# Four cond layers: ternary weights in two passes, chain scalars one per row, later waits for vectors, and other order tables for layers 0 and 1

## The chip, the cores and the metric

The kernel runs on one core of a Trainium2 chip. The metric is the time of one execution on the device in microseconds. The core has five engines with their own instruction streams: TensorE (PE, matrix products and transpositions), VectorE (DVE), ScalarE (ACT), GpSimd (POOL) and SyncE (SP, which issues most DMAs). They meet through semaphores.

## The reference

Input x has 8 examples of 512 tokens and 256 channels, and a condition vector of 256 for each example. Four layers follow one another on x. What matters here is layer 0 with its weights, and layer 1.

```
weight_quant(w): scale = 1 / max(mean|w|, 1e-5);  clip(round(w * scale), -1, 1) / scale
act_quant(x):    scale = 127 / max(max|x| over the row, 1e-5);  clip(round(x * scale), -128, 127) / scale
bitlinear(x, w, nw, b): xn = x * rsqrt(mean(x^2) + 1e-8) * nw;  act_quant(xn) @ weight_quant(w).T (+ b)

layer 0:  h = bitlinear(silu(c), wa0);  h = bitlinear(silu(gate) * y, wa2) with gate, y = bitlinear(h, wa1)
          h = rmsnorm(bitlinear(h, wa3) + ba3) * wr;  six vectors per example = bitlinear(h, wa4) + ba4
          mx = layernorm(x) * (1 + sc) + s;  i, f, g = bitlinear(mx, wi / wf / wg)
          o = scan(silu(i) * (1 - f), f) over the tokens;  x += gate_mix * bitlinear(rmsnorm(o) * silu(g), wo)
          x += gate_mlp * hgrn_mlp(layernorm(x) modulated)   with wm1 (256 to 2048) and wm2 (1024 to 256)
layer 1:  x += ffn(rmsnorm(merge(x, a mean of four tokens after pre_w, mixed with a style vector)))
```

So every weight matrix of layer 0 is made ternary (-1, 0 or 1, times its mean absolute value) by the kernel itself. wa0 to wa4 act on the 8 condition vectors, wi to wm2 on x. Layer 2 is an attention layer, layer 3 a state space layer; the change leaves both as they are.

## The kernel before

**Setup (`setup`, line 130).** SP loads wa0 to wa4 and then wi, wf, wg, wo, wm1, wm2 as f32, 128 partitions wide. A matrix is cut into pieces of at most 1536 columns (`pieces_of`). For each matrix ScalarE takes the sum of absolute values of each piece (`absolute`, L264) except for wm1, whose sums VectorE takes (L517). `inverse` (L374 to L378) adds up the pieces, lets TensorE sum over the partitions (L300) and makes the mean and its inverse. ScalarE multiplies the piece by the inverse (`scaled`, L270), VectorE adds and subtracts a large constant, which rounds (`whole`, L386), and then clips to -1 and 1 (`clipped`, L391). The codes are bf16.

Between these goes the chain of the condition: for each of wa0 to wa4 `front` (squares, multiplication with the norm vector, largest absolute value), `peak` (L424, L426), a power of -0.5 on GpSimd (L248), `quantised` (L435 to L446), the product on TensorE and `taken` (L453). The mean square, its root and the scales are tiles of 128 partitions and 8 columns, one column for each example, the same in each partition. The result, six vectors for each example, is written to DRAM (mod0).

**Layers 0 and 1 (`layers01`, line 583).** Both layers run in one block, example after example, in software pipelining. Five tables, `SP_TURN`, `POOL_TURN`, `ACT_TURN`, `PE_TURN` and `DVE_TURN`, each list the stages of its engine. An entry (stage, t, ahead) says that in turn b the engine does part t of that stage for example b + ahead. `steps` walks through the table turn by turn and leaves out examples that do not exist. An engine does its instructions in this order and waits at each for its semaphores. The stages of an example are, for layer 0: stats, root, xl, mx, ssq, rms, xw, amax, qs, xq (transposition), qT, proj, fi, scan, o, u, xo, yo, add1, x1; then the MLP with stats2 up to xq2, qT2, gate, up, silu, h, hq, qhT, y2, add2, x2; for layer 1: ssq3, xn, turn, xT, pre, z, fold, dots, s, base, merge, yn, turn2, hT, f1, gelu, f2, x3. The stage setup of layer 1 (harmonics, style) is done once, for example 0. On TensorE it is the first entry that has an example and waits for twelve small loads.

At the start of the block SP issues seven loads of norm vectors (ni, nf, ng, gn, no_, nm1, nm2), then mod_norm of example 0, the twelve small loads, and three weight loads. VectorE and GpSimd wait for all seven vectors before their first stage (L1145 and L742).

Of the kernel before, what the change touches and what calls it, by code (L numbers as in the profile page):

```python
# [11 lines left out]
P = 128  # L12
ALU = mybir.AluOpType
# [5 lines left out]
B, L, D = 8, 512, 256  # L19
# [96 lines left out]
WM1 = len(COND_W) + 4  # L116

# [7 lines left out]
def piece_number(i, j):  # L125

    return sum(len(pieces_of(q)) for q in range(i)) + j


def setup(nc, io, main, mean, ident, mod0, x_res, x_loaded):  # L130

    groups = COND_W + MAIN_W
    with ExitStack() as ctx:
# [11 lines left out]
        first4 = sb("first4", [P, PIECE], BF16)  # L145
# [11 lines left out]
        def codes(i, a, z):  # L157

            if i == 4:
                return first4[:] if a == 0 else raw4[:, a - PIECE:a].bitcast(BF16)[:, 0:PIECE]  # L160
            return (tern[i] if i < 4 else main[i - 5])[:, a:z]
# [4 lines left out]
        ones, half = sb("ones", [P, P]), sb("half", [P, B])  # L166
# [4 lines left out]
        sqk, pmax, ms, rms, s4, s6, s5 = [sb(name, [P, B]) for name in ("sqk", "pmax", "ms", "rms", "s4", "s6", "s5")]  # L171
        top, diag, own5, out_scale = sb("top", [B, 1]), sb("diag", [B, B]), sb("own5", [B, B]), sb("out_scale", [B, 1])
# [16 lines left out]
        def every(tile, k):  # L189
            return tile[:].rearrange("p (a b) -> p a b", a=1).to_broadcast([P, k, B])  # L190
# [4 lines left out]
        half_ready, ones_ready, ident_cleared, ident_ready = sem("half_ready"), sem("ones_ready"), sem("ident_cleared"), sem("ident_ready")  # L195
        abs_summed, abs_summed_v, asum_ready, total_ready, mean_ready, inv_ready = (
            sem("abs_summed"), sem("abs_summed_v"), sem("asum_ready"), sem("total_ready"), sem("mean_ready"), sem("inv_ready"))
        scaled_up, rounded, code_ready = sem("scaled_up"), sem("rounded"), sem("code_ready")
# [4 lines left out]
        top_ready, diag_ready, max_ready, ms_ready, rms_ready = (  # L203
            sem("top_ready"), sem("diag_ready"), sem("max_ready"), sem("ms_ready"), sem("rms_ready"))
        scale_step, s6_ready, s5_ready, qv_step, q_ready, y_ready, y_taken = (
            sem("scale_step"), sem("s6_ready"), sem("s5_ready"), sem("qv_step"), sem("q_ready"), sem("y_ready"), sem("y_taken"))
        tail_step, own_step, ba4_step, params_ready, stored = sem("tail_step"), sem("own_step"), sem("ba4_step"), sem("params_ready"), sem("stored")

        with nc.Block() as block:
            @block.sync  # L210
            def _(sp):
# [6 lines left out]
                a = 0  # L218
                for name, k in VECTORS:
                    sp.dma_start(rows[a:a + k, :], io["L0_cond_" + name].rearrange("(k p) -> k p", p=P)).then_inc(rows_loaded, 16)  # L220
                    a += k
                for i in (1, 2, 3):
                    weight(i)
# [6 lines left out]
                sp.wait_ge(rounded, piece_number(4, 0))  # L230
# [6 lines left out]
            def _(pool):  # L237
# [5 lines left out]
                                 pattern=[[-1, P]], channel_multiplier=1).then_inc(ident_ready, 1)  # L243
                gp.memset(half[:], -0.5).then_inc(half_ready, 1)
# [6 lines left out]
            def _(act):  # L251
# [3 lines left out]
                def absolute(i):  # L255
# [3 lines left out]
                    for j, (a, z) in enumerate(pieces_of(i)):  # L259
# [14 lines left out]
                absolute(0)  # L274
                scaled(0)
                absolute(1)
                absolute(2)
                scaled(1)
                scaled(2)
                absolute(3)  # L280
                act.wait_ge(h_ready, 2)
                ac.activation(h[:, 0:KA * B], h[:, 0:KA * B], ACT.Silu).then_inc(gate_ready, 1)
                scaled(3)
                absolute(4)
                scaled(4)
                for i in range(5, 9):
                    absolute(i)
# [2157 lines left out]
```

## Time and profile before

| what | us |
|---|---|
| median of 3 runs (2211.11 to 2214.26) | 2212.96 |
| the profiled execution's own time | 2210.04 |
| its span, first to last instruction | 2208.3 |
| TensorE busy | 1845.4 (84%) |
| VectorE busy | 1373.1 (62%) |
| ScalarE busy | 1121.4 (51%) |
| GpSimd busy | 601.9 (27%) |

The profile is one execution. "Busy" is the time in which an engine works on an instruction; a wait for a semaphore isn't busy. The timeline gives for each instruction its start, its duration, engine, line, the output and the inputs by tile names, and how long the engine was idle before it and who released it. Two times are told apart: the duration of an instruction, and the distance to the start of the next one, which is somewhat shorter where the next does not depend on it.

### The profile page before, as it was taken

How to read it: one execution, taken by the hardware profiler on the slowest of the kernel's cores; microseconds unless marked ns; L12 is line 12 of the kernel's file. 1: busy time of each engine (PE TensorE's matmuls, PEld its weight loads, DVE VectorE, ACT ScalarE, POOL GpSimd, SP SyncE). 2: the span in 40 equal slices, each digit the busy share in tenths (PEclk: the TensorE clock that was granted, in tenths of full speed). 3: DMA queues.
4: the chain of work that ended last, by engine and by line, in shares of the span. 5: the costliest groups of instructions: out<-in, count | busy, mean ns of one | idle time of the engine just before them, and what ended most of it. 6: DMA issues, size and time to landing. Idle time of an engine off the chain costs nothing. (4 is left out here: it accounts for less than half of the span.)

```text
span 2208.3 us, 26216 instructions
## 1 busy us (share of the span) xinstructions
PE 1845.4 (84%) x8726; PEld 1102.0 (50%) x8748; DVE 1373.1 (62%) x2936; ACT 1121.4 (51%) x2131; POOL 601.9 (27%) x774
## 2 busy tenths in 40 slices
PE   2244678988989997588999999999999857899998
PEld 1022445666666665422435454544544435566666
DVE  4647788798788642587776867686875205333331
ACT  7546567767767642215666665657576510121121
POOL 1056665565664421200001010110101100233322
PEclk9756799999999999759999999999999986899999
DMA  9310000000000001402112030202030011000000
GB/s 359 96 65 5 15 18 1 18 18 1 18 13 3 8 3 39 106 2 60 39 26 60 4 60 4 60 4 62 3 63 4 3 47 49 1 19 10 19 10 20
DMA packets 88313, 78.21 MB, mean 35 GB/s; under 512 B 9969, under 2 KB 82122, under 8 KB 87922
## 3 DMA queue, kind: packets, MB, share of 16 engines
q1 hardware_dynamic: 88178, 76.52, 12.7%
q8 instruction: 71, 1.16, 0.2%
q14 instruction: 64, 0.52, 0.1%
HBM read 46.67 MB, written 4.27 MB: 23 GB/s over the span
## 5 line engine op out<-in xcount | busy, mean ns | idle before, releaser
L1845 DVE TENSOR_REDUCE l_small<-l_psum 128x1 f32<-128x512 f32 x512 | 330.0, 685 | 135.3 <-PE l_psum L1792 130.8
L1604 ACT ACTIVATE l_prob<-l_psum 128x512 f32<-128x512 f32 x512 | 286.4, 596 | 227.2 <-PE l_psum L1662 223.9
L1792 PE MATMUL l_psum<-l_kT,l_qT 96*128 96x512 bf16 x512 | 191.3, 410 | 27.3 <-DMA l_kT<-l_early 12.2
L1662 PE MATMUL l_psum<-l_qT,l_kT 99*128 99x512 bf16 x512 | 174.4, 385 | 16.0 <-ACT l_prob L1604 14.3
L1588 POOL TENSOR_TENSOR k_x_res<-k_x_res,l_add 128x256 f32<-128x256 f32 x32 | 23.2, 726 | 466.9 <-DVE l_add L1889 466.9
L1671 PE MATMUL l_psum<-l_prob,l_v 128*32 128x512 f32 x1024 | 138.1, 612 | 0.2
L1792 PEld LDWEIGHTS l_psum<-l_kT,l_qT 96*128 96x128 bf16 x512 | 49.4, 98 | 171.1 <-DVE l_small L1845 116.6
L1736 PE MATMUL l_psum<-l_w,l_gu 128*128 128x256 f32 x512 | 133.9, 390 | 0.7 <-ACT l_gu L1620 0.7
L94 PE MATMUL l_psum<-l_hT,l_w 128*128 128x512 f32 x256 | 116.7, 606 | 8.6 <-ACT l_hT L2199 8.6
L94 PE MATMUL l_psum<-l_turned_over,l_w 128*128 128x512 f32 x256 | 120.3, 596 | 4.2 <-ACT l_gu L1620 4.2
L94 PE MATMUL l_psum<-l_hT,l_w_f 128*128 128x512 f32 x256 | 118.8, 600 | 2.7 <-ACT l_gu L965 1.7
L1125 PE MATMUL l_psum<-l_w_f,l_gu 128*128 128x256 f32 x512 | 120.1, 381 | 0.8 <-ACT l_gu L965 0.8
L94 PE MATMUL l_psum<-l_w,l_gu 128*128 128x256 f32 x512 | 111.9, 379 | 0.8 <-ACT l_gu L2203 0.8
L1736 PEld LDWEIGHTS l_psum<-l_w,l_gu 128*128 128x128 f32 x512 | 96.9, 195 | 19.2 <-ACT l_gu L1620 1.5
L94 PEld LDWEIGHTS l_psum<-l_w,l_gu 128*128 128x128 f32 x512 | 96.7, 190 | 14.4 <-ACT l_gu L2203 1.6
L1125 PEld LDWEIGHTS l_psum<-l_w_f,l_gu 128*128 128x128 f32 x512 | 94.1, 190 | 14.3 <-ACT l_gu L965 1.6
L1662 PEld LDWEIGHTS l_psum<-l_qT,l_kT 99*128 99x128 bf16 x512 | 46.4, 98 | 108.6 <-ACT l_prob L1604 63.4
L2203 ACT ACTIVATE l_gu<-l_psum,l_b 128x512 f32<-128x512 f32 x64 | 44.0, 687 | 96.2 <-PE l_psum L94 96.2
L94 PE MATMUL l_psum<-l_w_qkv,l_xT 128*128 128x512 f32 (+1 forms) x256 | 88.8, 490 | 3.2 <-DVE l_xn L1907 1.9
L2199 ACT ACTIVATE l_hT<-l_psum,l_shift,l_scale 128x512 f32<-128x512 f32 x16 | 11.7, 773 | 156.3 <-PE l_psum L100 156.2
L94 PEld LDWEIGHTS l_psum<-l_hT,l_w 128*128 128x128 f32 x256 | 48.4, 194 | 66.2 <-issue 55.6
L94 PE MATMUL l_psum<-k_t_wm,l_qT 128*128 128x512 bf16 x234 | 71.2, 406 | 10.8 <-DVE l_h L1260 3.4
(388 smaller groups left out, 3972.1 us busy)
## 6 DMA issues: line engine op xcount, KB each, us to landing
su_raw<-in_L_cond_wa SPq DMA_DIRECT2D x6, 1536.0 KB, 21.6
l_qT<-l_early SPq DMA_DIRECT2D x32, 192.0 KB, 3.6
l_kT<-l_early SPq DMA_DIRECT2D x32, 192.0 KB, 3.3
k_x_res<-in_x SPq DMA_DIRECT2D x1, 4096.0 KB
l_w<-in_L_cond_W SPq DMA_DIRECT2D x4, 1024.0 KB, 12.6
l_qT<-l_early SPq DMA_DIRECT2D x32, 128.0 KB, 3.2
l_kT<-l_early SPq DMA_DIRECT2D x32, 128.0 KB, 3.1
out<-k_x_res SPq DMA_DIRECT2D x8, 512.0 KB, 2.9
```

Source lines behind the costliest of these rows:

```text
L94: last = nc.tensor.matmul(out, w, m, start=(i == 0), stop=(i == len(pairs) - 1), **kw)
L1125: last = pe.matmul(psum[:, 6 + i % 2, 0:D], gu[:, f, tok(i)], w_f2[:, f, :], start=(f == 0), stop=(f == KF - 1))
L1588: pool.tensor_tensor(x_tile(e, n), x_tile(e, n), add2[:], ALU.add).then_inc(x_ready.sem, 1)
L1604: act.activation(prob[:, s % 2, j, :], psum[:, 2 + n % 2, :], ACT.Exp, scale=float(HD) ** -0.5).then_inc(exp_ready.sem, 1)
L1662: pe.matmul(psum[:, 2 + n % 2, :], kT[e % 2][:, head, tok(s % T)], qT[e % 2][:, head, :], start=True, stop=True).then_inc(st_ready.sem, 1)
L1671: last = pe.matmul(psum[j * BLOCK:(j + 1) * BLOCK, 4, :], v[e % 2][:, kt, at:at + BLOCK], prob[:, n % 2, j, :], start=(kt == 0), stop=(kt ...
L1736: last = pe.matmul(psum[:, mlp_bank(e, t), 0:D], gu[:, f, tok(t)], w_2[:, f, :], start=(f == 0), stop=(f == KF - 1))
L1792: pe.matmul(psum[:, n % 2, :], qT[e % 2][0:SROWS, n // T, tok(n % T)], kT[e % 2][0:SROWS, n // T, :], start=True, stop=True).then_inc(s_re ...
L1845: dve.tensor_reduce(mx[:, n % T, n // T:n // T + 1], psum[:, n % 2, :], AX.X, ALU.max).then_inc(max_ready.sem, 1)
L2199: act.activation(dst[:, k, :], psum[:, bank + k, :], ACT.Identity, scale=scale[:, k, bass.ds(nxt, 1)], bias=shift[:, k, bass.ds(nxt, 1)]). ...
L2203: act.activation(gu[:, n, :], psum[:, n % 2, :], ACT.Gelu_apprx_tanh, bias=b_1[:, n:n + 1]).then_inc(gu_ready.sem, 1)
```

## The change

**Setup.** For wa0 to wa3 VectorE does all of the ternary work in three passes: `whole` multiplies by the inverse mean and adds the large constant, in place and in f32; `low` subtracts it and takes the minimum with 1; `clipped` takes the maximum with -1. For wa4 and the weights of layer 0 VectorE does `whole`, and ScalarE takes the sign of the piece minus the constant (`sign`, with the tile `back` as bias), which is the code. The first two pieces of wa4 go to a tile of their own. VectorE takes the absolute sums of wm1 and wm2, between pieces of wa4. The inverses of wi, wf, wg and wo are made in one go. The norm vectors' seven row loads are issued by ScalarE instead of SP, before its first activation. In the chain the mean square, root and scales are now one value on each of 8 partitions; two diagonals (for the quantising scale and the output scale) are spread to all partitions by one product on TensorE (`scales`, `spread`). The mean square is taken before the largest value. x is loaded once `low` is through wa3.

**Layers 0 and 1.** mod_norm of example 0 is loaded first, then the seven vectors. VectorE waits for the three ifg vectors at the first xw and for the other four at the first xw2, GpSimd for these four at the first sgn. All five tables have the same stages in another order, with other values of ahead; layer 0 runs up to 4 turns ahead in place of 3, and ScalarE's table has gelu in two groups.

```diff
-                def scaled(i):
-                    act.wait_ge(inv_ready, i + 1)
-                    for a, z in pieces_of(i):
-                        ac.activation(raw[i][:, a:z], raw[i][:, a:z], ACT.Copy, scale=inv[:, i:i + 1]).then_inc(scaled_up, 1)
+                def sign(i):
+                    for j, (a, z) in enumerate(pieces_of(i)):
+                        act.wait_ge(rounded, piece_number(i, j) + 1)
+                        if i == 4 and j >= 2:
+                            act.wait_ge(signed, sign_number(i, j - 2) + 1)
+                        ac.activation(codes(i, a, z), raw[i][:, a:z], ACT.Sign, bias=back[:]).then_inc(signed, 1)
+                a = 0
+                for name, k in VECTORS:
+                    act.dma_start(rows[a:a + k, :], io["L0_cond_" + name].rearrange("(k p) -> k p", p=P)).then_inc(rows_loaded, 16)
+                    a += k
...
                 def whole(i, j):
                     a, z = pieces_of(i)[j]
-                    dve.wait_ge(scaled_up, piece_number(i, j) + 1)
-                    V.tensor_scalar(codes(i, a, z), raw[i][:, a:z], ROUND, ROUND, ALU.add, ALU.subtract).then_inc(rounded, 1)
+                    V.tensor_scalar(raw[i][:, a:z], raw[i][:, a:z], inv[:, i:i + 1], ROUND, ALU.mult, ALU.add).then_inc(rounded, 1)
+                def low(i, j):
+                    a, z = pieces_of(i)[j]
+                    dve.wait_ge(rounded, piece_number(i, j) + 1)
+                    V.tensor_scalar(codes(i, a, z), raw[i][:, a:z], ROUND, 1.0, ALU.subtract, ALU.min).then_inc(lowered, 1)
                 def clipped(i, j):
-                    V.tensor_scalar(codes(i, a, z), codes(i, a, z), 1.0, -1.0, ALU.min, ALU.max).then_inc(code_ready, 1)
+                    V.tensor_scalar(codes(i, a, z), codes(i, a, z), -1.0, None, ALU.max).then_inc(clipped_ready, 1)
...
+                def scales(i, n):
+                    step = Chain(dve, scale_step, i, 3)
+                    dve.wait_ge(top_ready, i + 1)
+                    dve.wait_ge(rms_ready, n + 1)
+                    step.link(V.tensor_tensor(s4[:], top[:], rms[:], ALU.mult))
+                    step.link(V.tensor_scalar(s4[:], s4[:], 1e-5, 1.0 / 127.0, ALU.max, ALU.mult))
+                    if i < 4:
+                        V.tensor_scalar(s5[:], s4[:], mean[0:B, i:i + 1], None, ALU.mult).then_inc(s5_ready, 1)
+                    step.link(V.reciprocal(s6[:], s4[:]))
+                    step.close()
+                    V.tensor_tensor(s6[:], s6[:], rms[:], ALU.mult).then_inc(s6_ready, 1)
+                    if i < 4:
+                        dve.wait_ge(s5_ready, i + 1)
+                        V.tensor_scalar(diag[:, B:2 * B], ident[0:B, 0:B], s5[:], None, ALU.mult)
+                    dve.wait_ge(s6_ready, i + 1)
+                    V.tensor_scalar(diag[:, 0:B], ident[0:B, 0:B], s6[:], None, ALU.mult).then_inc(diag_ready, 1)
...
-                dve.wait_ge(vectors_loaded, 16 * 7)
                 for stage, t, e in steps(DVE_TURN):
...
                     elif stage == "xw":
+                        if e == 0 and t == 0:
+                            dve.wait_ge(ifg_loaded, 16 * 3)
```

The order on VectorE from wa4 on is: three pieces, the inverses of wi to wo, three pieces, three absolute sums of wm1 each with a piece, the inverse of wm1, the last three pieces with the two sums of wm2 between, its inverse, then `whole` for all main weights with the three instructions of params after wm1. ScalarE's order is all absolute sums, then all signs. Of TensorE's new table for layers 0 and 1, the parts that the prediction speaks of:

```diff
+    ("f1", 4, -1), ("pre", 1, 0), ("xq2", 0, 1), ("proj", 2, 2), ("xq2", 1, 1), ("gate", 0, 1), ("f1", 5, -1), ("up", 0, 1), ("xq", 3, 2),
...
+    ("gate", 7, 1), ("fi", 2, 2), ("fi", 3, 2), ("up", 7, 1), ("merge", 1, 0), ("f1", 7, -1), ("o", 0, 2), ("o", 1, 2), ("merge", 2, 0), ("o", 2, 2),
+    ("o", 3, 2), ("f2", 0, -1), ("f2", 1, -1), ("hq", 0, 1), ("hq", 1, 1), ("merge", 3, 0), ("f2", 2, -1), ("setup", 0, 7), ("y2", 0, 1),
...
+    ("xq", 2, 3), ("f1", 1, 0), ("turn", 0, 1), ("f1", 2, 0), ("turn", 1, 1), ("f1", 3, 0), ("pre", 0, 1))
```

## Rows read from the trace of the kernel before

**Rows 1.** Instructions by line and shape, setup; busy us, mean ns | idle before.
```profile
L270 ACT ACTIVATE su_raw<-su_raw,su_inv 128x1536 f32<-128x1536 f32 x13 | 19.3, 1563 | 1.8 <-DVE su_inv L378 1.8
L264 ACT ACTIVATE su_junk<-su_raw 128x1536 bf16<-128x1536 f32 x13 | 19.3, 1481 | 0.7
...
L391 DVE TENSOR_SCALAR su_raw<-su_raw 128x1536 bf16<-128x1536 bf16 x11 | 6.0, 552 | 0.0
...
L517 DVE TENSOR_REDUCE su_parts<-su_raw_main 128x1 f32<-128x1536 f32 x2 | 3.5, 1738 | 0.0
```
**Rows 2.** Timeline of VectorE, the chain; start us, duration us, line, output and inputs.
```profile
25.78 0.28 DVE L453 TENSOR_TENSOR su_h<-su_t,su_s 128x112 f32<-128x112 f32 x1 [1.14 <-PE su_t L94]
...
38.07 0.15 DVE L411 TENSOR_SCALAR su_ms<-su_sum 128x8 f32<-128x8 f32 x1
40.03 0.17 DVE L435 TENSOR_TENSOR su_s<-su_all,su_rms 128x8 f32<-128x8 f32 x1 [1.82 <-POOL su_rms L248]
...
42.44 0.26 DVE L453 TENSOR_TENSOR su_h<-su_t,su_s 128x96 f32<-128x96 f32 x1 [0.83 <-PE su_t L94]
...
52.59 0.17 DVE L374 TENSOR_REDUCE su_asum<-su_parts 128x1 f32<-128x12 f32 x1 [3.36 <-ACT su_junk L264]
53.43 0.16 DVE L376 TENSOR_SCALAR k_all_mean<-su_total 128x1 f32<-128x1 f32 x1 [0.68 <-PE su_total L300]
```
**Rows 3.** Timeline of VectorE, first and last ternary work after the chain.
```profile
55.73 0.94 DVE L386 TENSOR_SCALAR su_first<-su_raw 128x1536 bf16<-128x1536 f32 x1
...
95.01 0.76 DVE L391 TENSOR_SCALAR k_t_wm<-k_t_wm 128x1536 bf16<-128x1536 bf16 x2
```
**Rows 4.** Stretches: length, busy PE, PEld, DVE, ACT, POOL, PE clock, DMA share, GB/s.
```profile
220.00:300.00 80.00, 52.39 (x261) 35.47 (x264) 65.94 (x122) 48.03 (x123) 49.41 (x63) 0.80 0.03 11
...
466.00:547.00 81.00, 73.63 (x373) 51.84 (x376) 68.64 (x130) 57.49 (x142) 50.54 (x65) 0.96 0.05 12
```
**Rows 5.** Timeline of VectorE, the scans of two examples following each other.
```profile
465.70 3.35 DVE L1194 TENSOR_TENSOR_SCAN l_si<-l_th,l_si 128x512 f32<-128x512 f32 x2
...
547.12 3.35 DVE L1194 TENSOR_TENSOR_SCAN l_si<-l_th,l_si 128x512 f32<-128x512 f32 x2
```
**Rows 6.** Waits of TensorE, 220 to 708 us; total us, times, longest.
```profile
PE l_psum L100 <- DVE l_si L1194: 12.5, 6, 2.4
PE l_psum L94 <- DVE l_qT L1184: 11.2, 18, 2.4
PE l_psum L100 <- ACT l_xT L938: 10.1, 6, 3.4
```
**Rows 7.** Timeline of GpSimd, a power on 8 and on 4 columns.
```profile
38.30 1.64 POOL L248 TENSOR_TENSOR su_rms<-su_ms,su_half 128x8 f32<-128x8 f32 x1 [6.05 <-DVE su_ms L411]
...
108.35 1.04 POOL L752 TENSOR_TENSOR l_small<-l_small 128x4 f32<-128x4 f32 x1
```
**Rows 8.** Line 1309; duration ns min/median/max, first and last start us.
```profile
L1309 DVE TENSOR_SCALAR l_w_f<-l_w_f,l_small x2: 734/734/734, 129.7 to 130.4; 128x1024 f32<-128x1024 f32 x2
```
**Rows 9.** Timeline of SP's queue, loads of row vectors.
```profile
1.73 1.60 SPq L220 DMA_DIRECT2D su_rows<-in_L_cond_na  x5
```
**Rows 10.** Timelines of SP, VectorE and TensorE at the start of layers 0 and 1.
```profile
96.85 0.35 SPq L692 DMA_DIRECT2D l_n_ifg<-in_L_cond_ni  x1
...
105.71 1.41 DVE L1152 BATCH_NORM_STATS2 l_small<-k_x_res 128x6 f32<-128x256 f32 x4 [8.67 <-DMA l_n_m<-in_L_cond_nm]
...
114.22 3.78 PE L1057 MATMUL l_psum<-l_gu 16*128 16x512 f32 x4 [25.58 <-DMA l_b_f<-in_L_cond_ffn_b]
117.93 1.88 PE L94 MATMUL l_psum<-l_small,l_gu 128*128 128x8 f32 x8
...
125.23 0.17 DVE L1297 COPY l_small<-l_psum 128x16 f32<-128x16 f32 x1
...
128.75 1.54 PE L100 MATMUL l_psum<-k_ident,l_xw 128*128 128x128 f32 x6
```
**Rows 11.** ScalarE by line, table loads before gelu.
```profile
L965 ACT ACT_TABLE_LOAD x7 | 9.0, 1283 | 0.1
```

More of the change, by code:

```diff
@@ L217, in _ @@
                 weight(0)
[L218 to L223, printed above, removed]
+                weight(1)
+                weight(2)
+                weight(3)
                 for c in range(0, K6, LOAD4):
@@ L253, in _, with absolute @@
                 done = 0
-                def absolute(i):
+                def absolute(i, first, end):
                     nonlocal done
@@ L258, in absolute @@
                         act.wait_ge(loaded[i], 16)
-                    for j, (a, z) in enumerate(pieces_of(i)):
+                    for j in range(first, end):
+                        a, z = pieces_of(i)[j]
                         if i == 4 and j % LOAD4 == 0:
@@ L360, in _ @@
                 last.then_inc(y_ready, 1)
-                for i in range(5, len(groups)):
-                    total(i)
             @block.vector
@@ L398, in ternary @@
+                def ternary(i, first, end):
+                    for j in range(first, end):
                         whole(i, j)
-                        clipped(i, j - 1)
-                    clipped(i, n - 1)
+                        if j > first:
+                            clipped(i, j - 1)
+                        low(i, j)
+                    clipped(i, end - 1)
                 def squared(k, n):
@@ L459, in _ @@
                 dve.wait_ge(cols_ready, 1)
+                inverse(0)
                 dve.wait_ge(silu_ready, 1)
                 front(0, 0)
-                ternary(0)
-                peak(0, 0)
+                peak(0)
+                ternary(0, 0, 1)
+                scales(0, 0)
                 quantised(0, 0)
@@ L507, in _ @@
-                ternary(4)
-                dve.wait_ge(loaded[WM1], 16)
-                for j, (a, z) in enumerate(pieces_of(WM1)):
-                    if j == 1:
+                V.tensor_scalar(s5[:], s4[:], mean[0:B, 4:5], None, ALU.mult).then_inc(s5_ready, 1)
+                for j in range(3):
+                    whole(4, j)
+                inverse(5, WM1 - 5)
+                for j in range(3, 6):
+                    whole(4, j)
+                for j in range(3):
+                    absolute(WM1, j)
+                    whole(4, 6 + j)
@@ L511, in _ @@
+                inverse(WM1)
+                whole(4, 9)
+                absolute(10, 0)
+                whole(4, 10)
+                absolute(10, 1)
+                whole(4, 11)
+                inverse(10)
+                for i in range(5, len(groups)):
+                    for j in range(len(pieces_of(i))):
+                        whole(i, j)
+                    if i == WM1:
                         dve.wait_ge(y_ready, 5)
-                        dve.wait_ge(own_step, 2)
+                        dve.wait_ge(s5_ready, 5)
@@ L1158, in _ @@
                     elif stage == "xw":
+                        if e == 0 and t == 0:
+                            dve.wait_ge(ifg_loaded, 16 * 3)
                         dve.wait_ge(mx_ready.sem, mx_ready.at(e, t + 1))
```

265 lines of the change are left out of this document (130 added, 135 removed), and 31 rows, old and new, of tables (ACT_TURN, PE_TURN, POOL_TURN).

## The prediction

> **What bounds the kernel now.** I read the profile in this order: the busy shares by stretch, then the timelines of each engine over the setup (0 to 97 us) and over the first stretch of the two layers, then the waits of TensorE in the steady part. The program has four stretches: weight setup to 96.85 us, layers 0 and 1 together to 873.5, layer 2, layer 3. The change touches the first two only.
>
> In the setup TensorE is nearly idle; the clock is held by a chain that runs through VectorE and ScalarE. ScalarE takes absolute sums (1.48 us for 1536 columns) and then scales (1.56 us for 1536), VectorE rounds and then clips (0.55 us) [rows 1]. The chain of small operations hands on the result of its second product at 25.78 and of its fourth at 42.44, and waits 3.36 us for the absolute sum of wa4 at 52.59 [rows 2]. The large ternary work begins on VectorE at 55.73, with a rounding of 0.94 us, and ends with the row of 95.01, which ends at 95.77 [rows 3].
>
> In the steady part of layers 0 and 1 TensorE is busy 73.6 of 81 us; before that, from 220 to 300, it is busy 52.4 of 80 [rows 4]. One turn (an example) takes 81.4 us there, scan to scan [rows 5]. So TensorE is the nearest bound of a turn, and what is to be won there is some 7 us a turn of waits. Of these the wait for qT is 11.2 us and the wait for xT 10.1 us over six turns [rows 6].
>
> **Part 1, the chain of wa0 to wa4.** *Scalars one per row.* In stage 3 the mean square stands at 38.07, behind peak and diagonal, and the scales at 40.03 [rows 2]: 1.96 us for a GpSimd power of 1.64 us on 8 columns. The trace has no power on one column. A power on 4 columns takes 1.04 [rows 7]; a line through both gives 0.6 for one column, an estimate. Bounds: 0.6 and 1.64; I take 0.6. The mean square also comes before the peak now, so the power runs beside the transposition of the maxima. That takes about 1.5 us out of a stage. Against it, three more VectorE steps of 0.2 and a TensorE spreading (0.4 us longer than the steps it replaces) now stand behind the power: +1.0. Net -0.5 per stage.
>
> *Ternary by VectorE alone.* Each piece of wa0 to wa3 now takes three passes on VectorE: multiply and add (f32 in place), subtract and min, max. In place on f32 with a per-row scalar, 1024 columns take 0.734 us [rows 8], nearly as fast per column as the present rounding (0.94 for 1536, the last 0.06 of it beside the next instruction); so I price 1536 columns at 0.88 from start to start, and the piece at 0.88 + 0.88 + 0.59 = 2.35 where VectorE spent 1.47 and ScalarE 1.56 beside it. wa0 to wa3 have 8960 columns: about +5.1 us on VectorE, and these pieces no longer lie under a long power.
>
> *Loads.* The seven row vectors go out on ScalarE's queue ahead of its table load and first activation. On SP's queue five took 1.60 us, 0.32 each [rows 9]; the trace has none on ScalarE's, so 2.4 us in front of ScalarE's first work is the estimate, up to 4 if dearer there. wa1 gets issued 2.4 us earlier for it. The absolute sums then run without the scaling between them and finish near 43 instead of 52.4, as the loads permit: the wait of 3.36 at 52.59 is gone.
>
> Laying these steps one behind another on VectorE (0.21 for a dependent small step, 0.84 for a trip to TensorE and back, the 52.59 and 53.43 of rows 2, and 1.2 for a weight mean), the chain hands on at 29.0 (before 25.78) and 46.6 (42.44). So it is 4 us late there: 0.8 from the start, 5.9 for the third pass and what lay under the powers, less 2.2 for the stages' scalars, and the weights' pieces of wa1 now all stand before its own product is fetched. It wins back the 3.36 of the wait and part of two powers, and VectorE starts on wa4 at 57.6, 1.9 us later than 55.73.
>
> **Part 2, wa4 and the weights of layer 0.** From there VectorE does one pass per piece and ScalarE the sign. VectorE: twelve pieces of wa4 at 0.88 = 10.6; the main weights' 8192 columns = 5.0; absolute sums of wm1 and wm2 (1.74 for 1536, rows 1) = 4.5 + 2.3; three inverses 0.55 + 1.2 + 1.2; params 2.0 as now. Sum 27.3 us. ScalarE: the trace has no Sign. Its nearest rows are Abs from f32 to bf16 (1.48 busy, 1.39 to the next) and Copy (1.56 busy, some 1.47 to the next) [rows 1]. With 1.4 the twelve pieces take 16.8 and the rest 8.2: 25.0, beginning 1 us after VectorE. So both engines are about even, VectorE last, and one wide and one narrow sign trail its last pieces by 2 us: 29.5 us in all, against 40.0 before (55.73 to 95.77). The setup ends at 57.6 + 29.5 = 87.1. **Gain 8.6 us.** Bounds: 12 if the chain loses nothing, 2 if ScalarE needs 1.56 a piece and its queue loads are dear. TensorE follows wa4 at 0.8 to 1.4 us a piece and is covered.
>
> **Part 3, vectors awaited at first use.** Now VectorE's first statistics wait until 105.71 for seven vectors, 8.7 us of it idle, after the barrier at 96.85 [rows 10]. They go now at once, mod_norm is the first load, and the three ifg vectors are wanted only by xw, which comes after statistics, root, normalising and mx. But TensorE's first work waits for the twelve small loads, until 114.22, 17.4 us after the barrier, and this queue is as long as before: that wait stays. What shortens is behind it: the harmonics and style products end at 119.8 (117.93 + 1.88), and VectorE copies the style only at 125.23, since it had the late qs to do first. With statistics 8.7 us earlier it stands ready. The first transposition for layer 0, at 128.75, moves to 5.2 us nearer the barrier (the 5.4 between 119.8 and 125.23, less a hand-over). **Gain 5.2 us**, bounds 0 (something of the same queue, such as w_pre, is late next) and 8.7.
>
> **Part 4, the other tables.** Every table has the same stages in another order and the same work. By position, fi to f2(7) lies 3.66 turns apart on TensorE (3.27 before), and xq comes 0.50 turns ahead of fi (0.35). A deeper pipeline gives each hand-over more room and costs at the ends. I went through the waits: proj used to follow its xq by one or two products, and now three or more lie between; hq has two f2 blocks before it; turn(1) still has one f1 block between, so the xT wait may stay. The scan wait (12.5 us in six turns) stays: up(7), merge(1), f1(7) cover about what merge, f2 and hq did. Of 3.6 us a turn for qT and xT I take a third as won, 1.2; over seven turns **8 us**. Bounds: all 7 us a turn won, -45; and two table loads a turn lost, below, +20.
>
> ScalarE now has gelu in two groups (0 to 4, then 5 to 7) with proj and silu between: four table loads a turn instead of two. One takes 1.283 us, and before gelu there are 7 in the eight turns now, one each [rows 11]. ScalarE is busy 57.5 of 81 [rows 4], so 2.6 us more has cover, except at f1(7), which waits for gelu(5): up(7) and merge(1), 2.6 us, stand against fi, load and gelu, 2.7. Cost 0.3 a turn, inside the third above.
>
> The Trainium skill ("ScalarE: Activation LUTs", Rules for kernel authors) tells one to do all of one table set before switching, and budgets some 2.7 us a switch. The rule is against this table; the trace's load is half its figure. By its figure ScalarE would carry 5.4 us more a turn, by the row 2.6.
>
> **Sum.** The profiled execution took 2210.04 (span 2208.3); the median shown is 2212.96, 2.9 above it. 2210.0 - 8.6 - 5.2 - 8 = 2188.2, and with the 2.9 the median should be 2191. I say 2192. Layers 2 and 3 begin at a barrier and keep their time.
>
> **Rivals.** *A, only the setup counts.* The tables give nothing: the scan wait and the order of examples hold the turn at 81.4, as they did from 220 to 300 us, where the turn was already about 80 long and TensorE busy only 65% [rows 4]. Time 2199, and with 0.5 to 1 us a turn lost 2203 to 2208. *B, the tables do more.* With proj, hq and turn waits all gone a turn is 77 to 78: 7 x 4 = 28 instead of 8, time 2172. For it: most waits are hand-overs of under 2.5 us. Against: 200 to 300 us was not bound by TensorE either.
> *C, slower.* Both added table loads of each turn fall on TensorE's path, one before proj(2), which xq(3) waits for, one before gelu(5), which f1(7) waits for: 2 x 1.283 x 8 = 20.5 us, more than the 13.8 of parts 1 to 3; time 2220. It decides from 1.7 us a turn on. ScalarE's 24 us a turn of idle time speak against it. (The Trainium skill's rule on table sets, above, points this way.)
> *D, the scaling in place is slow.* If multiply and add ran at the rate of the reduction (1.74 for 1536), the 26624 columns of wa4 and the main weights would cost 0.85 more per 1536: +15 on these alone, the gain of the setup is gone, and the time is 2206. The row of 0.734 speaks against.
>
> **Chances.** Forecast (tables -3 to 0 a turn) 0.52; A 0.20; B 0.13; C 0.08; D or another cover lost 0.07. The measurement tells 0.2%, 4.4 us, from no change. Faster 0.84, within 0.09, slower 0.07. Range 2173 to 2211: B's far part and C are left out.
>
> **What would show it.** VectorE's first wa4 pass near 57.6, with no wait for an absolute sum; the power of 0.6 us; signs of 1.4 to 1.5; the last sign near 87; bn_stats within 1 us after the barrier; TensorE's first xw transposition 26.7 us after the barrier instead of 31.9; scan to scan 80 us; four table loads a turn. Wrong would be: the setup's end later than 92, TensorE waiting for gelu or proj over 1 us each turn, or a turn above 82.

## The result, and the profile after

The changed kernel takes 2154.76 us (median; 2151.69 to 2156.48), the kernel before beside it on the same chip 2213.61. The ratio is 0.9731, 95% interval 0.9712 to 0.975: 58.9 us less. The prediction said 2192, so it named the right sign and missed the size by 37 us; 2154.8 lies below its range too. The profiled execution has a span of 2154.3 us at a mean granted clock of 0.913, the same as before.

The weight setup ended when it was forecast to. These are rows of VectorE, ScalarE, GpSimd and TensorE from the timelines of the changed kernel (start, duration, line, output and inputs, and in brackets the idle time before):

```profile
9.28 0.21 DVE L494 COPY su_cols<-su_t 128x49 f32<-128x49 f32 x1 [9.28 <-PE su_t L100]
...
47.45 0.26 DVE L490 TENSOR_TENSOR su_h<-su_t,su_out 128x96 f32<-128x96 f32 x1 [0.90 <-PE su_t L94]
...
49.24 0.54 POOL L254 TENSOR_TENSOR su_rms<-su_ms,su_half 8x1 f32<-8x1 f32 x1 [5.24 <-DVE su_ms L439]
...
55.64 0.16 DVE L393 TENSOR_REDUCE su_asum<-su_parts 128x1 f32<-128x12 f32 x1
...
57.00 1.93 DVE L409 TENSOR_SCALAR su_raw<-su_raw,su_inv 128x1536 f32<-128x1536 f32 x2
...
85.21 2.19 ACT L280 ACTIVATE k_t_wm<-su_raw_main,su_back 128x1536 bf16<-128x1536 f32 x2 [0.68 <-DVE su_raw_main L409]
...
88.71 1.41 DVE L1199 BATCH_NORM_STATS2 l_small<-k_x_res 128x6 f32<-128x256 f32 x4
...
105.73 3.77 PE L1105 MATMUL l_psum<-l_gu 16*128 16x512 f32 x4 [23.58 <-DMA l_b_f<-in_L_cond_ffn_b]
...
111.35 0.17 DVE L1348 COPY l_small<-l_psum 128x16 f32<-128x16 f32 x1 [3.43 <-PE l_psum L94]
...
114.88 1.43 PE L100 MATMUL l_psum<-k_ident,l_xw 128*128 128x128 f32 x6
```

The absolute sum at 55.64 is no longer waited for (3.36 us in [rows 2]); wa4 starts at 57.00 (55.73 in [rows 3]); the last sign ends at 87.40 and the barrier stands at 88.48 (96.85 in [rows 10]); the first transposition for layer 0 comes 26.4 us behind the barrier (31.9 before). The pieces of 1536 columns, grouped by line and shape over the setup (the engine's busy us and mean ns, then idle time), answer to [rows 1]:

```profile
L280 ACT ACTIVATE su_raw<-su_raw,su_back 128x1536 bf16<-128x1536 f32 x10 | 15.1, 1566 | 1.8 <-DVE su_raw L409 1.8
L409 DVE TENSOR_SCALAR su_raw<-su_raw,su_inv 128x1536 f32<-128x1536 f32 x13 | 12.8, 1010 | 0.1
```

What did not come out as forecast is layers 0 and 1. VectorE's scans, which mark the turns, stand here:

```profile
420.18 2.33 DVE L1243 TENSOR_TENSOR_SCAN l_si<-l_th,l_si 128x512 f32<-128x512 f32 x2
...
494.26 2.33 DVE L1243 TENSOR_TENSOR_SCAN l_si<-l_th,l_si 128x512 f32<-128x512 f32 x2
```

In [rows 5] a pair of scans took 3.35 us; it takes 2.33 now. And two turns, from scan to scan, with the columns of [rows 4], from the kernel before:

```profile
382.61:465.70 83.09, 75.19 (x374) 53.08 (x376) 69.29 (x131) 57.73 (x143) 50.94 (x65) 0.94 0.04 12
465.70:547.12 81.42, 73.89 (x374) 51.84 (x376) 69.06 (x131) 57.91 (x143) 50.96 (x65) 0.96 0.05 12
```

and from the changed kernel:

```profile
347.45:420.18 72.73, 70.57 (x376) 51.05 (x377) 62.30 (x131) 60.38 (x145) 46.57 (x64) 0.98 0.05 14
420.18:494.26 74.08, 72.09 (x376) 52.48 (x377) 60.86 (x127) 60.42 (x145) 46.48 (x64) 0.95 0.05 13
```

TensorE is busy 71.3 us of a turn in the mean. Before it was 74.5 in these two turns and 73.6 in [rows 4], and I had read that number as a floor. VectorE's busy time fell from 69.2 to 61.6 a turn. Four of its statistics instructions lie outside the second stretch (x127 instead of x131), which is 0.7 of this; so VectorE is about 6.9 us shorter for the same instructions. GpSimd's fell from 50.9 to 46.5, also for the same instructions. That is the reading that the prediction lacked.

From first to last of the eight scans it was 552.1 us (156.35 to 708.45) and is 496.3 (142.03 to 638.34). The time from the last scan to the end of layers 0 and 1 grew from 164.7 to 174.8, as a deeper pipeline that empties would have it. So the 59.9 us between the two profiled executions at the end of layers 0 and 1 (873.1 and 813.2, the last x3) are 14.3 up to the first scan, 55.8 between scans, and -10.2 behind them. Layers 2 and 3, the same in all kernels here, took 1335 to 1341 us in the profiled executions. They were 5.9 us longer in the changed kernel's, so that its span is only 54.0 shorter.

TensorE's waits over two turns of the changed kernel (347.5 to 494.3; total us, times, longest) answer to [rows 6]; scan, xT and the large qT waits are gone:

```profile
PE l_psum L94 <- ACT l_gu L1013: 2.5, 4, 0.9
PE l_psum L94 <- issue: 0.4, 2, 0.2
PE l_psum L94 <- DVE l_qT L1304: 0.2, 1, 0.2
```

### The profile page after: what moved, and what is told of

The parts are those of the page before. It is cut to its first block and busy times, and to the rows that moved or that the text cites. A ratio compares the mean times of both kernels' runs of the same rounds, so it can differ in the third digit from the quotient of the medians.

```text
span 2154.3 us, 26196 instructions
## 1 busy us (share of the span) xinstructions
PE 1839.9 (85%) x8728; PEld 1104.3 (51%) x8744; DVE 1328.7 (62%) x2922; ACT 1121.0 (52%) x2127; POOL 568.9 (26%) x775
## 5 line engine op out<-in xcount | busy, mean ns | idle before, releaser
L1843 PE MATMUL l_psum<-l_kT,l_qT 96*128 96x512 bf16 x512 | 192.2, 412 | 27.1 <-DMA l_kT<-l_early 12.1
L1713 PE MATMUL l_psum<-l_qT,l_kT 99*128 99x512 bf16 x512 | 175.6, 388 | 16.0 <-ACT l_prob L1655 14.3
L1713 PEld LDWEIGHTS l_psum<-l_qT,l_kT 99*128 99x128 bf16 x512 | 46.5, 98 | 108.3 <-ACT l_prob L1655 63.0
```

Source lines behind the costliest of these rows:

```text
L1713: pe.matmul(psum[:, 2 + n % 2, :], kT[e % 2][:, head, tok(s % T)], qT[e % 2][:, head, :], start=True, stop=True).then_inc(st_ready.sem, 1)
L1843: pe.matmul(psum[:, n % 2, :], qT[e % 2][0:SROWS, n // T, tok(n % T)], kT[e % 2][0:SROWS, n // T, :], start=True, stop=True).then_inc(s_re ...
```

## The experiments

All times are medians, each beside runs of the kernel before on the same chip (2212 to 2213 us); ratios are to that kernel, with 95% intervals. A turn is the mean of four, from the third scan to the seventh.

**1. Tables alone.** Edit: in the kernel before, only the five tables replaced.

```
 # kernel before, with
-SP_TURN, POOL_TURN, ACT_TURN, PE_TURN, DVE_TURN as before
+SP_TURN, POOL_TURN, ACT_TURN, PE_TURN, DVE_TURN of the changed kernel
```

> The kernel before with the five new tables and nothing else of the change. Theory T (the tables carry most of the gain: from the two traces, first to last scan fell from 552 to 496 us, and the run-out after the last scan grew by 10): 45 us less than before, 2168; a turn of 72 to 73 us, TensorE's waits for scan, qT and xT all but gone. Rival S (the turn became short only because the setup and the late vectors changed how layers 0 and 1 start): above 2180, a turn of 78 or more. The recorded forecast (tables worth 8): 2205.

Measured: 2170.89, ratio 0.9809 (0.9795 to 0.9823), 42.2 us less; turn 72.9, scans 2.33. Theory T stands: the tables carry it, and need nothing of the new setup.

**2. Setup and late vectors, old tables.** Edit: the changed kernel with the five old tables.

> The changed kernel with the five old tables: new weight setup and late waits for vectors alone. Theory T: the 13.9 us that parts 1 to 3 of the prediction give, 2199 to 2200, setup's end at 87.4 and the first xw transposition near 115, a turn of 80 to 83 as before. Rival S: 2190 or less, the turn shortens here too. If this gain and that of the tables alone don't add up to 59, the parts help or hinder each other.

Measured: 2199.96, ratio 0.9936 (0.9922 to 0.9949), 13.2 us less; turn 82.5; first xw transposition at 114.93. The prediction's 13.9 for parts 1 to 3 is confirmed. 42.2 and 13.2 make 55.4 of the 58.9; the 3.5 that are left lie within what the intervals leave open.

**3. Late vectors alone.** Edit, in the kernel before, beside the new order of the loads:

```
-                pool.wait_ge(vectors_loaded, 16 * 7)
-                dve.wait_ge(vectors_loaded, 16 * 7)
+                        if e == 0 and t == 0:          # in xw
+                            dve.wait_ge(ifg_loaded, 16 * 3)
+                        if e == 0 and t == 0:          # in xw2, and GpSimd's sgn
+                            dve.wait_ge(vectors_loaded, 16 * 4)
```

> The kernel before with nothing but the late waits: mod_norm loaded first, the ifg vectors awaited by xw, the others at their own first use; old setup, old tables. Theory (part 3 of the prediction): 5.2 us less, 2208, first xw transposition 26.5 us after the barrier instead of 31.9. Rival: the fill of the pipeline has slack and takes the 5 us back before the first scan or the second, within 2 us of before.

Measured: 2208.56, ratio 0.9978 (0.9969 to 0.9988), 4.5 us less; the first xw transposition at 122.69 instead of 128.75. Part 3 (5.2) holds, and the setup alone is left with 8.7.

**4. GpSimd beside the scan.** Edit in the changed kernel:

```
                         pool.wait_ge(ssqh_ready.sem, ssqh_ready.at(e, t + 1))
+                        if t == 2:
+                            pool.wait_ge(h_ready.sem, h_ready.at(e, 2 * T))
                         gp.tensor_tensor(h[:, t, :], h[:, t, :], n_m2[:], ALU.mult)...
```

> The changed kernel, where GpSimd's multiplication of h tile 2 (128x1024, 2.4 us) waits until the last piece of h is done, so that it runs beside VectorE's two scans as GpSimd's work did before the change, instead of just ahead of them. No work added. Theory C (the two engines slow each other, and a good part of the shorter turn is that the new order keeps GpSimd off the scan): a scan grows from 1.21 to about 1.7, the multiplication from 2.4 to 3.3, and the turn by 1 us or more, 2162 or above. Rival P (TensorE bounds the turn now, VectorE has 10 us of slack): the scan grows likewise, the turn does not, within 3 us of the changed kernel's 2155.

Measured: 2167.73, ratio 0.9786 (0.9772 to 0.9801), 13 us more than the changed kernel; turn 75.3. Theory C, and more strongly than it said. From the timelines of VectorE and GpSimd of this run:

```profile
424.67 4.45 DVE L1245 TENSOR_TENSOR_SCAN l_si<-l_th,l_si 128x512 f32<-128x512 f32 x2
...
424.89 3.14 POOL L855 TENSOR_TENSOR l_h<-l_h,l_n_m 128x1024 f32<-128x1024 f32 x1 [4.17 <-DVE l_h L1313]
```

The first scan takes its 1.22 us. GpSimd's instruction, started 0.2 us later, is 0.77 longer than the 2.37 that it takes in the changed kernel: it waits for the first scan. The second scan, 3.3 us, ends 1.1 us behind GpSimd's instruction, that is, it ran almost wholly once that was over. So the two engines take turns here, by whole instructions. The edit also makes the multiplication later (GpSimd stands idle 4.17 us ahead of it), and no run separates this from the collision. But over two turns of this run no wait for the multiplication is among the longer ones of any engine, while TensorE again waits for the scan (1.3 us). With this in mind the same is to be seen in the kernel before, beside the scan of 465.70 in [rows 5], where GpSimd's instructions of 256 columns take 1.52 and 1.64 instead of 0.73:

```profile
464.77 0.73 POOL L761 TENSOR_TENSOR l_mx<-l_mx,l_mod_norm 128x256 f32<-128x256 f32 x1
465.45 0.92 POOL L760 TENSOR_TENSOR l_mx<-l_mx,l_mod_norm 128x256 f32<-128x256 f32 x1
466.45 1.52 POOL L761 TENSOR_TENSOR l_mx<-l_mx,l_mod_norm 128x256 f32<-128x256 f32 x1
467.94 1.64 POOL L769 TENSOR_TENSOR l_sg<-l_sg,l_gn 128x256 f32<-128x256 f32 x1
```

An operation of four columns pays the whole price too; VectorE and GpSimd of the kernel before:

```profile
443.00 2.27 DVE L1349 TENSOR_SCALAR l_small<-l_small 128x4 f32<-128x4 f32 x1
...
442.90 2.35 POOL L805 TENSOR_TENSOR l_h<-l_h,l_n_m 128x1024 f32<-128x1024 f32 x1
```

In the changed kernel the same step (L1400) takes 0.17 (the second number is the mean ns of one):

```profile
L1400 DVE TENSOR_SCALAR l_small<-l_small 128x4 f32<-128x4 f32 x2 | 0.3, 170 | 0.1
```

The Trainium skill ("GPSIMD Engine Reference", 1. Specifications) says that GpSimd shares its SBUF interfaces with VectorE, and contends with instructions that have two SBUF inputs or run in a mode with two ports. The traces agree as far as they go: VectorE's scans (two SBUF inputs) are stretched, while its reductions of 128x1024 stay at 1.21, and its scalar_tensor_tensor with a PSUM input, 128x512, at 0.75, in both kernels. The step of four columns has one input; in which mode it ran, no run here shows.

**5. The scan freed in the kernel before.** Edit, in GpSimd's mx:

```
                         pool.wait_ge(xl_ready.sem, xl_ready.at(e, t + 1))
+                        if e and t == 3:
+                            pool.wait_ge(scanned.sem, scanned.at(e - 1, 1))
```

> The kernel before, old tables, where GpSimd's last mx of the next example waits for VectorE's scan, so that no GpSimd work runs beside it. Nothing else changed, no work removed. Theory C (beside each other the two engines take turns, and the scan lies on the path): both scans 1.20 each (2.33 for two instead of 3.35), TensorE's wait for them 1.4 instead of 2.4 us a turn, the turn 0.5 to 1 us shorter, 2206 to 2210. Rival G: GpSimd, 50.9 us busy of 81, is now late with what follows (mx, sgn, xo) and VectorE waits for that instead: 2213 or more.

Measured: 2208.84, ratio 0.9981 (0.9972 to 0.9991), 3.7 us less; all scans 2.33; turn 81.3 instead of 82.0. A wait added, and the kernel is faster. Theory C; but it removes one collision of many (VectorE is still busy 68.7 us a turn).

**6. GpSimd made light, old tables.** Edit, in ten places of GpSimd's part, all alike:

```
-   ...gp.tensor_tensor(mx[:, t, :], mx[:, t, :], mod_norm[:, 1, :], ALU.mult)...
+   ...gp.tensor_tensor(mx[:, t, 0:16], mx[:, t, 0:16], mod_norm[:, 1, 0:16], ALU.mult)...
```

> The kernel before, old tables, where GpSimd's ten elementwise stages in layers 0 and 1 (mx, mx2, sgn, xo, x1, x2, xb, hw) touch 16 columns instead of 256 or 1024, so that nearly all of GpSimd's time and of its collisions with VectorE is gone (the rest of those tiles is left out of the computation). Theory C (collisions of the two engines make a good part of the old turn): VectorE's busy time a turn falls from 69 to near 62, the turn from 81 to 75 or less, 2170 or less. Rival H (the order of hand-overs makes the old turn, whatever GpSimd does): VectorE's busy time falls likewise, the turn stays at 78 or more, 2195 or more.

Measured: 2149.47, ratio 0.9708 (0.9693 to 0.9723), 62.5 us less; turn 73.7, VectorE busy 61.4.

**7. The same, new tables.**

> The same leaving out in the changed kernel, new tables. Both theories: TensorE bounds the new turn (70.5 of 72.7 busy), so it gets shorter by 1 us at most, 2145 to 2155. If it fell below 2140, GpSimd would still be holding the new turn. The distance between this run and the same edit of the kernel before is what the tables give without GpSimd: some 13.9 for the setup and then 10 or less by theory C, 30 or more by H.

Measured: 2142.7, ratio 0.9683 (0.9669 to 0.9696), 12.1 us less than the changed kernel; turn 71.9. Between 6 and 7 are 6.8 us, and the new setup with the late vectors was worth 13.2 in run 2: without GpSimd's load the new tables gain nothing over the whole, they lose some 6 us. From the first to the last scan they give 10.9 us (495.2 and 484.3), and behind the last scan they take 16.7 (161.5 and 178.1). So nearly all that the tables give hangs on GpSimd's load. This is Theory C or K: the edit takes away GpSimd's collisions and its length together.

**8. Both at one length: GpSimd as long as before, but narrow, old tables.** Beside the edit of 6, each stage is followed by a power on one column (two on four columns behind hw):

```
+   def idle(columns):
+       ...
+       return gp.tensor_tensor(extra[:, 1 + padding % 2, 0:columns], extra[:, 0, 0:columns], half[:, 0:columns], ALU.pow)
```

> The kernel before, old tables, GpSimd's elementwise stages on 16 columns as in light_gpsimd_before, but each now followed by a power on one column (0.55 us; two powers on four columns behind hw, 2.1 us), so that GpSimd is about as long at each stage as before while it touches almost none of the memory that VectorE works on. Theory C (collisions): VectorE's busy time stays near 62 us a turn, the turn at 76 or less, 2165 or less. Rival K (the light run was fast because GpSimd's results came sooner, not because it was out of VectorE's way): the turn is back at 79 or more, 2195 or more, with VectorE's busy time near 62 all the same. If VectorE's busy time is back at 66 or more, the power itself is in its way, and the run doesn't tell the two apart.

Measured: 2186.83, ratio 0.9878 (0.9862 to 0.9895), 26.5 us less; turn 77.6. The stretches of two turns:

```profile
374.50:450.83 76.33, 71.58 (x374) 50.59 (x376) 61.65 (x132) 57.94 (x143) 51.52 (x105) 0.98 0.04 13
450.83:528.46 77.63, 73.05 (x374) 52.10 (x377) 61.64 (x131) 58.04 (x143) 50.97 (x105) 0.96 0.04 13
```

GpSimd is busy 51 us of a turn, as in the kernel before; VectorE 61.6, as in the changed one. So this is the old order with VectorE freed of its collisions, but with GpSimd as long as it was with them, and the time lies between what C and K expected: neither alone.

**9. The same, new tables.**

> The same edit in the changed kernel, new tables: GpSimd as long as before at each stage, almost nothing touched. Theory C: the turn stays at 71.8 as in light_gpsimd_after, 2143 to 2150. Rival K: 2153 or more, because the 12 us that the light run gained came from GpSimd's shorter stages.

Measured: 2160.57, ratio 0.9762 (0.9747 to 0.9777), 5.8 us more than the changed kernel; turn 75.0. Rival K is right in this: GpSimd's durations count. With the wait behind each narrow operation it is busy 48.1 here against 46.5, and the turn is 2.1 longer than the changed kernel's with VectorE no busier. With the same edit the old order has 51.2, so some 3 us a turn of GpSimd's lengthening are still in run 8. The edit thus has a cost of its own and leaves a part of the collisions in; I take the 26.5 us of run 8 as a lower bound of what the collisions cost the old order, and the 62.5 of run 6, which also makes GpSimd's stages short, as an upper one.

**10. Cover ahead of the scan's wait.** Edit in the old table of TensorE:

```
-    ("hq", 0, -1), ("o", 0, 0), ("o", 1, 0), ("hq", 1, -1), ("merge", 3, -2),
+    ("hq", 0, -1), ("hq", 1, -1), ("merge", 3, -2), ("o", 0, 0), ("o", 1, 0),
```

> The kernel before with two entries of TensorE's table moved: hq(1) and merge(3), 2.2 us of products, stand ahead of o(0) and o(1), which wait for the scan, instead of behind them. Theory W (TensorE's waits are what a turn is above its work, and cover ahead of a wait removes it): the 2.4 us a turn of waiting for the scan fall to 0.5 or less, the turn to 79.5 or less, 2201 or less. Rival V (the cycle through VectorE and ScalarE holds the old turn, and TensorE's waits only move): the scan's wait falls, but waits for qT, xT, h or sg grow by as much, 2211 or more.

Measured: 2225.47, ratio 1.0052 (1.0038 to 1.0065), 13.5 us slower; turn 84.2. TensorE waits at another place:

```profile
467.42 3.35 DVE L1194 TENSOR_TENSOR_SCAN l_si<-l_th,l_si 128x512 f32<-128x512 f32 x2
...
471.18 0.48 DVE L1367 SCALAR_TENSOR_TENSOR l_xn<-l_psum,l_small,l_xn 128x256 f32<-128x256 f32 x1
471.72 1.13 PE L94 MATMUL l_psum<-l_w_merge,l_xT 128*128 128x256 f32 x4 [2.89 <-DVE l_xn L1367]
```

The product merge(3) needs VectorE's merge(2), which stands behind the scan on VectorE. So of the 2.2 us that were moved only hq(1), some 0.4, could run ahead of the scan, and the rest waits longer than o(0) did. The wait moved, as rival V says, and grew. The run shows that products counted by position are no cover when they hang on the same late engine; what 2 us of products that are free to run would win was not tested.

**11. No change of ScalarE's table.** Edit in the changed kernel, L1013; the GELU of layers 0 and 1 is replaced by SiLU:

```
-   ac.activation(gu[:, t, :], psum[:, 6 + t % 2, :], ACT.Gelu, bias=b_f1[:, t:t + 1])...
+   ac.activation(gu[:, t, :], psum[:, 6 + t % 2, :], ACT.Silu, bias=b_f1[:, t:t + 1])...
```

> The changed kernel where the GELU of layers 0 and 1 is replaced by the SiLU that the same layers already use, so that ScalarE never changes its table there (the values differ, the work on every other engine is the same): 4 table loads of 1.28 us a turn are gone. Theory T (ScalarE has 12 us of idle time a turn and the loads are covered but for part of TensorE's 1.25 us a turn of waits for gu): 3 to 7 us less than the changed kernel, 2148 to 2152. Rival L (two groups of GELU cost what they add, the price that the new order pays): 15 us or more less, 2140 or below.

Measured: 2149.6, ratio 0.9714 (0.9698 to 0.9729), 5.2 us less than the changed kernel (the two intervals overlap), turn 72.7 instead of 72.9. Theory T. Spread over eight turns all four loads together cost at most some 0.6 us a turn, and TensorE's waits for gu (2.5 us in two turns, above) are gone.

**12. Row vectors on SP's queue.** Edit in the changed kernel's setup:

```
                 weight(0)
+                for name, k in VECTORS:
+                    sp.dma_start(rows[a:a + k, :], ...).then_inc(rows_loaded, 16)
                 weight(1)
...
-                for name, k in VECTORS:
-                    act.dma_start(rows[a:a + k, :], ...).then_inc(rows_loaded, 16)
```

> The changed kernel with the seven row vectors issued on SP's queue behind wa0, as before the change, instead of on ScalarE's. Theory R (the rows that land 3.4 us later than before hold up the whole chain): rows land near 5.6, VectorE starts near 6 instead of 9.28, the setup ends 2 to 3 us earlier, near 85, and the time is 2152. Rival: the loads of wa1 to wa4, issued 2.4 us later, or ScalarE's sums are what the chain waits for further on: setup's end within 1 us of 87.4, time 2154 to 2156.

Measured: 2150.52, ratio 0.9718 (0.9705 to 0.9731), 4.2 us less than the changed kernel (the two intervals overlap a little). TensorE has the rows at 5.35 instead of 8.94 and VectorE starts at 5.70 instead of 9.28; the first statistics of layer 0 come at 85.43 instead of 88.71, and the last x3 at 809.2 instead of 813.2: 3.3 of the 3.6 us reach the end of the setup. The edit changes the queue and also puts the rows ahead of the loads of wa1 to wa4; which of the two makes them land sooner, this run doesn't tell.

**13. TensorE's first loads ahead of the later vectors.** Edit in the changed kernel: gn, n_o, n_m1, n_m2, b_merge and b_f2 are issued behind the ten small loads that TensorE's first products need, and its wait is for these ten.

> The changed kernel, at the start of layers 0 and 1: the loads that TensorE's first products need go straight behind mod_norm and the three ifg vectors; gn, n_o, n_m1, n_m2, b_merge and b_f2 follow behind them, awaited at their first use. Theory: TensorE's first products begin near 101 instead of 105.7, the first xw transposition near 110 to 111 instead of 114.9, 4 us less, 2151. Rival: VectorE's statistics, quantisation factors (done at 107.2) and the later vectors hold the fill, or slack in it takes the gain back before the second scan: 2154 to 2156.

Measured: 2155.38, ratio 0.9734 (0.9717 to 0.9752), no difference. The first products begin at 98.89 instead of 105.73, the first xw transposition at 111.61 instead of 114.88, the scans mostly 2 us earlier (from 0.4 to 2.1); the last x3 begins at 814.5 instead of 813.2. The rival. In the profiled execution the gain is lost behind the last scan: that part takes 178.1 us instead of 174.8; the longer waits of TensorE are the same, but it is busy 3.6 us more, at a granted clock of 0.95 instead of 0.97. In run 14, which has the same edit, that part takes 174.8 at 0.97. So the loss lies in the clock of that execution, and the time (2148.3 to 2157.6 in four) is too uneven to show 2 us.

**14. Both.**

> The changed kernel with both reorderings of loads: row vectors on SP's queue behind wa0, and TensorE's first loads of layers 0 and 1 ahead of the later vectors. If the two add up: 4.3 less for the first (measured alone) and some 2 for the second (its scans came 1.3 to 2 us earlier alone, though the time did not show it): 2149. Rival: the second gives nothing in the time, 2150.5, or its later vectors cost where the start is earlier, 2152.

Measured: 2147.01, ratio 0.9705 (0.9692 to 0.9719). This version is 65 us below the kernel before. Its interval reaches that of run 12 by itself and touches the changed kernel's; in the traces the last x3 begins at 808.1 instead of 813.2, of which run 12 alone has 4.0.

The runs that bear on the turn, side by side (VectorE busy a turn from the stretches between scans):

```
                                    turn, us   VectorE busy   whole program, us
before                               82.0        69.2          2213
changed                              72.9        61.6          2154.8
tables alone                         72.9        61.6          2170.9
setup and late vectors alone         82.5        69.2          2200.0
before, scan freed                   81.3        68.7          2208.8
before, o later                      84.2        69.4          2225.5
before, GpSimd narrow                77.6        61.6          2186.8
before, GpSimd light                 73.7        61.4          2149.5
changed, GpSimd narrow               75.0        60.2          2160.6
changed, GpSimd light                71.9        60.1          2142.7
changed, GpSimd beside scan          75.3        63.6          2167.7
```

## Why the prediction was right and wrong

**Part 1, right in its end, by sizes off that nearly cancel.** VectorE starts wa4 at 57.00 (57.6 forecast). On the way there the chain hands on at 31.08 (29.0 forecast) and at 47.45 (46.6), and the sums of wa4 end at 47.8 on ScalarE (43), so a part of the agreement is luck. The prediction's own parts for this stretch, 0.8 + 5.9 - 2.2, also make 4.5 and not the 4.2 that it used. A power on one column takes 0.54 (0.6 forecast), though once 1.57 when VectorE works beside it. Multiplying and adding in place takes 1.01 busy and, two back to back in 1.93, about 0.93 from start to start (0.88). The loads of the row vectors took 2.7 us on ScalarE's queue, near the 2.4 of the estimate, but I counted only what they put in front of ScalarE. They also land later: VectorE's first work waits for them until 9.28, and run 12 prices that at 3.3 us of setup and 4.2 of the whole.

**Part 2, right.** 30.4 us (57.00 to 87.40) for 29.5: the sign takes 1.57 busy and 1.46 to the next (1.4 forecast). The last one ends at 87.40 (87.1): the stretch is 0.9 longer and began 0.6 earlier. The gain at the setup's end is 8.4 (8.6). Rival D is out: in place it takes 1.01, not 1.74.

**Part 3, right.** 5.5 between the traces, 4.5 alone in run 3, 5.2 forecast. The small loads still hold TensorE 17.25 us behind the barrier.

**Part 4, wrong: this is the step that failed.** It said that "TensorE is the nearest bound of a turn, and what is to be won there is some 7 us a turn of waits", and took a third of the waits for qT and xT, 8 us in all. The tables alone gave 42.2 in place of the 8, just inside the bound of 45 (all 7 us of waits over seven turns would be 49). Three things were wrong in it.

*The floor.* I took TensorE's busy time, 73.6, for work that no order can change. In the new order it is 71.3 for the same products, and a turn, 72.9, is shorter than the supposed floor. A part of it goes with the granted clock: at 0.96 and 0.95 it is 73.9 before and 72.1 after, so 1.8 us are left between stretches of like clock. Single groups changed both ways (the transpositions of xw from 313 to 273 ns in the mean, the products of proj from 274 to 308), so what sets their length is not shown.

*The cause of the waits.* I looked at which hand-over each of TensorE's waits named, counted the products that cover it in the new table, and found the scan's cover unchanged and turn(1) still with one block of f1. The count was right and beside the point. Run 10 adds 2.2 us of cover by such a count, most of which itself hangs on VectorE, and makes the kernel slower. What made results late was in good part VectorE and GpSimd in each other's way: against the new order VectorE lost about 6.9 us a turn and GpSimd 4.4. Both numbers stood in the profile before as instructions of one shape with different durations: GpSimd's 256 columns at 0.73 in one place and 1.5 in another, a four-column step of 2.27, and the scan pair of 3.35 in [rows 5], where the last of the eight took 2.33. I read the durations as costs of operations.

*How much is the collisions'.* A turn fell by 9.1 us. The collisions cost the old order at least 4.4 (82.0 to 77.6, run 8) and at most 8.3 (82.0 to 73.7, run 6, where GpSimd's shorter stages help as well). With GpSimd's work light or narrow the new tables give 1.8 (runs 6 and 7) to 2.6 (runs 8 and 9) a turn, near the 1.2 forecast; so 6.5 to 7.3 of the 9.1 need GpSimd's full work to appear. How this splits into collisions and GpSimd's own length stays open: no run takes the collisions away and leaves each GpSimd duration exactly as it is.

**Table loads, right in size.** Run 11 puts all four at 0.6 us a turn at most; the forecast was 0.3 for the two added. TensorE's wait is at f1 behind gelu, where the prediction had it. It is 1.25 us a turn, above the 1 us that the prediction had named as a sign of being wrong; with the wait gone (run 11) the turn is 0.2 shorter, so this sign told little. Rival C is out. By the Trainium skill's rule ("ScalarE: Activation LUTs", Rules for kernel authors) the switches should have been avoided; in this order nearly all of them are covered by ScalarE's idle time, and a load is 1.28 us in the trace.

**Rivals.** A fell with run 1. B had the direction with 28 us, by waits that vanish, and I gave it 0.13 because "200 to 300 us was not bound by TensorE either". That sentence held the answer: TensorE was 65% busy there, VectorE 82%, and [rows 4] showed it.

## What to carry to other kernels

Before pricing a new order of instructions, group the instructions of VectorE and GpSimd by shape and compare the shortest with the mean. What the mean has above the shortest may be collision: look at what the other engine did at these times. If it is, order alone can win it, and it is missing from every count of operations. Where waits of the busiest engine name many different partners, ask what makes the partners late rather than put cover in front of each wait. And a load that is issued sooner need not land sooner: look at the landing, not at the issue, of a load that a chain begins with.

## What the runs showed of the hardware

VectorE's scan over 128x512 in f32 takes 1.21 us alone and up to 3.3 beside one GpSimd instruction of 2.4: these two exclude each other for whole instructions, in both directions, and an instruction of four columns waits as long as a large one (2.27 instead of 0.17). VectorE's reductions of 128x1024 keep their 1.21 us. Seven small loads cost 2.7 us in front of ScalarE's first instruction, and their data, issued from 0.73 us on beside the large loads of wa1 to wa3, were there 3.6 us later than from SP's queue, where they were issued from 1.73 us on and ahead of these (run 12). A wait added to GpSimd made a kernel faster (run 5), and an instruction of 2.4 us moved to beside a scan made another 13 us slower (run 4).
